# Expert batches of 6, 5, 3 and 2 groups in units of 128 rows, with seven weight slots, in a GNN and mixture-of-experts layer

## What is computed

```python
z = layernorm(x)
msg = z @ W + B
weights = where(adj < 1, exp(-(1/adj - 1)**2 / 0.5), 0)
x = x + weights @ msg
z = layernorm(x)
logits = z @ gate_w + gate_b
vals, idx = top_k(logits, 2)
share = softmax(vals)
h = relu(z @ w1[e] + b1[e])
expert_out = h @ w2[e] + b2[e]
y = z + sum(share * expert_out[idx])
x = x + layernorm(y) * gamma + beta
```

## Time and profile before

| what | value |
|---|---|
| median of three runs | 1759.18 us (1758.34 to 1759.6) |
| the profiled execution | 1758.88 us, its span 1757.1 us |
| PE, DVE, ACT, POOL busy | 92%, 87%, 90%, 24% of the span |
| aggregation until the last sum is copied | 0 to about 1470 us |
| tail | from there to 1757.1 us |
| rows loaded, a unit of 256 or of 128 | 128 KB in 2.1 us, 64 KB in 1.8 us from issue to landing |
| copy of one expert's weights | 493 ns, 120 times |

### The profile page before, as it was taken

How to read it: one execution, slowest core, us unless ns; L and a number is a source line. 1 busy time by engine, 2 the same in 40 slices (tenths; PEclk the granted TensorE clock), 3 DMA queues, 4 the chain that set the end, 5 groups by cost and what they waited for, 6 DMA issues and landing times.

```text
span 1757.1 us, 23405 instructions
## 1 busy us (share of the span) xinstructions
PE 1624.8 (92%) x8178; PEld 1080.6 (61%) x8178; DVE 1525.8 (87%) x2278; ACT 1581.2 (90%) x1577; POOL 430.1 (24%) x309
## 2 busy tenths in 40 slices
PE   4889999999999999999999999999999999999840
PEld 3556666566656566656556656566656557999840
DVE  7999999999999999999999999999999994557876
ACT  5889999999999999999989999999999995666752
POOL 0000030303131313131304030303031301117775
PEclk9999999999999999999999999999999999999985
DMA  9447876667666666666867666667666842457653
GB/s 319 146 136 252 251 213 205 187 203 217 200 203 199 195 204 204 202 200 201 230 192 207 203 207 204 189 202 216 203 188 203 230 123 77 149 156 227 193 152 97
DMA packets 208500, 341.91 MB, mean 195 GB/s; under 512 B 18224, under 2 KB 65840, under 8 KB 208256
## 3 DMA queue, kind: packets, MB, share of 16 engines
q1 hardware_dynamic: 200064, 323.30, 61.9%
q0 software_dynamic: 8320, 17.12, 3.2%
HBM read 304.38 MB, written 35.98 MB: 194 GB/s over the span
## 4 chain that ended last, share of the span: by engine, by line
PE 44%; ACT 28%; DVE 12%; issue 11%; POOL 4%; DMA 1%; POOLq 0%; SPq 0%; DVEq 0%; ACTq 0%
PE acc L1033 22%; PE tp L1052 11%; ACT chunk L467 10%; ACT chunk L462 9%; ACT wT L473 8%; PE tp L1082 4%; PE tp L1095 4%; POOL chunk L446 4%; DVE chunk L595 4%; DVE chunk L589 4%; PE tp L1071 1%; PE misc L985 1%; DVE stats L601 1%; DVE msg L650 1%; DMA xs<-in_x_dram 1%
## 5 line engine op out<-in xcount | busy, mean ns | idle before, releaser
L1033 PE MATMUL acc<-wT,msg 128*128 128x512 f32 x2048 | 973.0, 598 | 16.2 <-DVE yT L681 16.2
L595 DVE SCALAR_TENSOR_TENSOR chunk<-chunk 128x2048 f32<-128x2048 f32 x256 | 585.6, 2287 | 98.2 <-ACT chunk L467 98.0
L1052 PEld LDWEIGHTS tp<-ident,chunk 128*128 128x128 f32 x4096 | 484.1, 142 | 226.2 <-issue 214.7
L473 ACT ACTIVATE wT<-tp 128x1024 f32<-128x1024 f32 x512 | 570.4, 1114 | 22.4 <-PE tp L1052 22.4
L589 DVE SCALAR_TENSOR_TENSOR chunk<-chunk 128x2048 f32<-128x2048 f32 x256 | 584.0, 2282 | 1.9 <-DMA chunk<-in_adj_dram 1.9
L1052 PE MATMUL tp<-ident,chunk 128*128 128x128 f32 x4096 | 538.5, 275 | 0.0
L462 ACT ACTIVATE chunk<-chunk 128x2048 f32<-128x2048 f32 x256 | 514.9, 2011 | 11.9 <-DVE chunk L589 11.9
L1033 PEld LDWEIGHTS acc<-wT,msg 128*128 128x128 f32 x2048 | 351.6, 192 | 267.7 <-issue 267.0
L467 ACT ACTIVATE chunk<-chunk 128x2048 f32<-128x2048 f32 x256 | 513.7, 2007 | 0.0
L418 POOL TENSOR_TENSOR pool_carrier<-pool_carrier 1x1 f32<-1x1 f32 x32 | 8.6, 270 | 1232.0 <-DVE row_now L766 1189.5
L428 POOL DMA_INDIRECT rows_in<-y,row_now x128 | 286.6, 2239 | 44.7 <-issue 44.7
(11 more groups left out here) (106 smaller groups left out, 574.8 us busy)
## 6 DMA issues: line engine op xcount, KB each, us to landing
chunk<-in_adj_dram SPq DMA_DIRECT2D x256, 1024.0 KB, 5.3
chunk<-rows_in SPq DMA_DIRECT2D x88, 128.0 KB, 2.1
rows_out<-chunk SPq DMA_DIRECT2D x88, 128.0 KB
y_kept<-y SPq DMA_DIRECT2D x16, 256.0 KB, 6.1
rows_in<-zeros SPq DMA_DIRECT2D x32, 128.0 KB
chunk<-y_kept SPq DMA_DIRECT2D x16, 256.0 KB, 3.4
out_dram<-chunk SPq DMA_DIRECT2D x16, 256.0 KB, 2.6
blobs<-in_L_ffn_w_dram SPq DMA_DIRECT2D x1, 2048.0 KB, 12.0
```

The source lines that it names most:

```text
L473: act.activation(wT[:, (g * PPG + m) % WSLOTS, :], tp[(g * PPG + m) % TSLOTS][:, :], ACT.Exp, scale=-2.0).then_inc(weighted, 1)
L595: dve.scalar_tensor_tensor(out=slot(c), in0=slot(c), scalar=2.0, in1=slot(c), op0=ALU.subtract, op1=ALU.mult).then_inc(squared, 1)
L1033: ins = pe.matmul(acc[:, :], msg[:, n, :], wT[:, (g * PPG + m) % WSLOTS, k * ROWS:(k + 1) * ROWS], start=(n == 0), stop=(n == 2 * PPG - 1))
L1052: ins = pe.transpose(tp[s % TSLOTS][:, t * ROWS + b * P:t * ROWS + (b + 1) * P], chunk[:, c % RING, b, j:j + P], ident[:, :])
```

## The change

The batches become 6, 5, 3 and 2 groups, all in units of 128 rows, and each batch has 15 spare units for partly filled ones instead of 16. There are seven weight slots and weights are copied five units ahead, twelve slots for loaded rows instead of eight, and six result slots instead of four. The last group's gate takes a step only in every second round; its table begins in round 55, its pads in round 74. Groups are combined from 14 rounds behind a batch's last unit on, eleven rounds apart. Since a batch's number of units is no longer a multiple of the result slots, the wait for the results counts each slot's stores by itself.

```diff
--- before.py
+++ after.py
@@ -41,15 +41,15 @@
 
 
 
-    BATCHES = (8, 6, 2)
-    TILES = (2, 2, 1)
+    BATCHES = (6, 5, 3, 2)
+    TILES = (1, 1, 1, 1)
     UR = [t * P for t in TILES]
     UW = max(UR)
     FIRST = [sum(BATCHES[:b]) for b in range(len(BATCHES) + 1)]
     assert FIRST[-1] == GROUPS
     REGION = [n * ROWS + u for n, u in zip(BATCHES, UR)]
     BASE = [sum(E * r + u for r, u in zip(REGION[:b], UR)) for b in range(len(BATCHES) + 1)]
-    UNITS = [K * n * ROWS // u + E for n, u in zip(BATCHES, UR)]
+    UNITS = [K * n * ROWS // u + E - 1 for n, u in zip(BATCHES, UR)]
     UNIT0 = [sum(UNITS[:b]) for b in range(len(BATCHES) + 1)]
     NU = UNIT0[-1]
     MOST = max(UNITS)
@@ -134,7 +134,7 @@
         e_tab = sb("e_tab", [1, NU], I32)
         r_tab = sb("r_tab", [1, NU], I32)
 
-        SLOTS, RIN, RT, HT, RO, BACK, ZS, FIN = 4, 8, 3, 3, 4, 4, 3, 2
+        SLOTS, RIN, RT, HT, RO, BACK, ZS, FIN = 7, 12, 3, 3, 6, 4, 3, 2
         ring = chunk[:, :, :, :].rearrange("p r b j -> p (r b j)")
 
         def carve(start, n, width):
@@ -229,20 +229,16 @@
         MISC = 4
         SETUP_MISC = 2
 
-        def batch_at(i):
-            return max(b for b in range(len(BATCHES)) if UNIT0[b] <= i)
-
-
-        GATE_PACE = 1
-        TABLE_AT, PADS_AT = 28, 47
+
+        GATE_PACE = 2
+        TABLE_AT, PADS_AT = 55, 74
         TAIL_TABLES = len(BATCHES) - 1
-        COMBINE_WAIT, COMBINE_PACE, COMBINE_LONG = 8, 6, 10
+        COMBINE_WAIT, COMBINE_PACE, COMBINE_LONG = 14, 11, 10
         starts = []
         for b, n in enumerate(BATCHES):
             for _ in range(n):
                 at = UNIT0[b + 1] + COMBINE_WAIT
-                pace = COMBINE_PACE if starts and UR[batch_at(starts[-1])] > P else COMBINE_LONG
-                starts.append(max(at, starts[-1] + pace) if starts else at)
+                starts.append(max(at, starts[-1] + COMBINE_PACE) if starts else at)
         LAST = starts[-1] + COMBINE_LONG + 2
 
         def batch_of(u):
@@ -431,7 +427,7 @@
 
             def results_there(b):
                 for i in range(RO):
-                    pool.wait_ge(ro_out[i], UNIT0[b + 1] // RO * 16)
+                    pool.wait_ge(ro_out[i], (UNIT0[b + 1] - i + RO - 1) // RO * 16)
 
             for b, n in enumerate(BATCHES):
                 for g in range(FIRST[b], FIRST[b + 1]):
@@ -945,14 +941,14 @@
                     dve.tensor_tensor(fin[g % FIN], z, rows(xs, g), ALU.add).then_inc(fin_ready, 1)
 
             dve.wait_ge(turned, (GROUPS - 1) * PPG + PPG - RING // 2 * PAIRS)
-            for u in range(2):
+            for u in range(SLOTS - 2):
                 fetch(u)
             gate_sum(GROUPS - 1)
             for i in range(LAST):
                 if 1 <= i <= NU:
                     add_bias(i - 1)
-                if i + 2 < NU:
-                    fetch(i + 2)
+                if i + SLOTS - 2 < NU:
+                    fetch(i + SLOTS - 2)
                 if i % GATE_PACE == 0:
                     gate_slot(GROUPS - 1, i // GATE_PACE)
                 table_slot(len(BATCHES) - 1, i - TABLE_AT)
```

## The result

The change makes the kernel slower: 1769.76 us, median of four runs (1768.24 to 1773.7), against 1759.39 (1758.34 to 1759.76) for the kernel before beside it. The ratio is 1.0065 [1.0049, 1.0081]. The prediction was 1752 us, range 1741 to 1764, so the time lies outside the range and on the other side of no change. The profiled execution took 1768.24 us, its span 1766.3.

What follows compares the result with a forecast made beforehand. The tail was taken as bound by sync queue and VectorE, both without room: first bias 1477.4, last bias 220 us later at 1697.4, 52.5 us of combine, 1.8 outside the span: 1752 us, range 1741 to 1764.

Steps and rivals of the forecast that it cites:

- part 3: Tail units: the sync queue's 1.00 us per unit plus table reads and pads sum to F + 212.3.
- F: Time of the tail's first bias, forecast at 1477.4 us; later tail times are counted from it.
- Part 1: Tables built in the aggregation, three batches' instead of two: 3.8 us more in sum, 2 to 6 kept.
- Part 2: Start of the tail: half as tall a tile takes about 1.0 us off before the first bias (0 to 2).
- The interference of 3.5 us: Tail units: sync queue and VectorE, each without room, lose 3.5 us to each other; last bias F + 220.
- VectorE's own pace: Tail units with the combine beside them: 13.0 us per 11 units, 1.18 each; last bias F + 216.4.
- Part 4: Tail: gathers start at 1551, 21 us sooner; 52.5 us remain after the last bias, without waiting for gathers.
- gathers were not starved: Against the rival that every VectorE copy blocks GpSimd 0.49 us: gathers end 1784, program near 1799 us; chance 0.02.
- Results that return too slowly: Rival, tail: stores take 6.5 us to land, so six slots hold biases back; F + 237.7, 1769 us; chance 0.13.
- The queue overlaps: Rival, tail: the queue hides; TensorE's 75.2 us to round 73, then 1.12 per unit; F + 202, 1734 us; chance 0.15.
- No change: Rival: tables cost 6 us, queue and VectorE cost each other 8; 1759 us; chance 0.18.
- three signs of being wrong: Tail: queue under 1.00 us per round, biases waiting 6 us for stores, or the last combine group waiting for its gather.

Runs made afterwards that it cites:

- e1: The changed kernel with twelve result slots instead of six; 1765.24 us, ratio 1.0038 to the kernel before.
- e4: The changed kernel with the last batch's 16 pads in rounds 57 to 72 instead of 74 to 89; 1767.86 us, ratio 1.0064 to the kernel before.
- f1: e1 with the results of two neighbouring units in one store of 128 KB; 1745.21 us, ratio 0.9934 to the kernel before.
- f2: f1 with a transfer of 512 bytes for each left-out store; 1756.66 us, ratio 0.9998 to the kernel before.
- f4: f1 with a combine group every nine rounds instead of 11; 1746.76 us, ratio 0.9932 to the kernel before.

## Why the prediction was wrong

**What bounds the kernel, and where to look: right.** The aggregation kept TensorE's pace, and only the tail decided. The step that failed is the queue's own sum in part 3, F + 212.3 for the store of unit 181, which was issued at F + 236.8. Against the span of 1749.9 the profiled one is 16.4 longer: F came 6.4 us sooner (1471.0 for 1477.4), the units took 23.3 us more (F + 243.3 for F + 220), and the rest 0.5 less.

**Part 1, tables: too dear.** Forecast 3.8 us more, measured -2.3. The first table cost 4.1 us where 5.4 was forecast, that of group 12 3.0 for 4.4, and the last two groups gave 0.4 back where I had 1.4 of cost. Another 1.3 us was already there at the first sum, and is not the change's. One profile cannot tell more: in six profiles of kernels with this aggregation (after, e1, e4, f1, f2, f4) the last sum is copied between 1468.33 and 1473.87, mean 1470.7.

**Part 2, first bias: right.** 1.3 us sooner for a forecast of 1.0.

**Part 3, the queue's own sum: wrong, and the cause of the miss.**

| the queue's round | forecast | store issued |
|---|---|---|
| 73 (unit 72) | F + 78.4 | F + 86.8 |
| 89 (unit 88) | F + 106.1 | F + 117.5 |
| 182 (unit 181) | F + 212.3 | F + 236.8 |

The unit's 1.00 and the pad's 0.53 us were right. Two terms were not. The long issues were put at nothing: 20 of them add 16 us. The table reads were put at 0.87 us, 13 times, from a load of 1.21 us that was in truth one of the long issues. They are instructions of their own in the gap ahead of a load:

```profile
L332 SPq TENSOR_LOAD <-r_tab x15: 278/1033/2132, 1442.4 to 1687.3; - x15
```

The three figures are the least, the median and the longest in ns. 14 of these and one for the pads lie in the units. There are more than the multiples of 16 give, since each batch begins with a read too. With their gaps they take 17 us, where 11 was forecast. The two terms together are 22 of the 24.5 us; waits for results before that store are 3.3, and six rounds without a load give 1.8 back.

Both costs stood in the trace of the kernel before, with 8 long issues and reads of the same length. They cost nothing there, because that queue spent 77.9 us waiting for results.

**The interference of 3.5 us: not what failed.** The queue lost 1.2 us to VectorE up to unit 177 and 5.9 in the last stores. VectorE lost 24.4 us to the queue, but that is the queue's pace reaching it through six slots. With twelve, the queue's work stayed at 238 us and so did the length of the units. With half the stores it fell to 218.0 - 33.1 = 184.9 us and the last bias came at F + 218.0. VectorE's own pace was nearly right: 1.18 a unit forecast, 1.215 measured in f1, where the queue has room, and last bias F + 218.0 against my F + 216.4.

**Part 4, gathers and combine: right in the main, partly by luck.** GpSimd started at 1548.2 for 1551, but by two errors that cancel: the last store of the first batch was issued at F + 74.1, not F + 67, and released GpSimd 3.1 us later, not 6.5. It paused between batches (17.2 us before the second), and the rest after the last bias took 52.0 for 52.5 us with one wait of 2.1 for a gather. That gathers were not starved is right too: five groups from 1548.18 to 1602.16 took 10.80 us each, against the 10.91 and 10.34 of the earlier trace rows (10.88 and 10.40 from marker to marker). The rule of the Trainium skill, "SBUF — State Buffer", section "SBUF: two separate sides", can have cost some 0.4 us a group here at most.

**The rivals.** *Results that return too slowly* gave 1769 us, and bias 89 at F + 108.8 (measured F + 108.7). The number is right by luck: the stores seen to hold a bias landed within 1.9 to 4.6 us of their issue, not 6.5, but were issued up to 10 us after the result. *The queue overlaps* fell with the 1.00 us between stores. *No change* let queue and VectorE cost each other 8 us, where 7.1 were the queue's waits, but took the queue's sum as I did. None of the rivals, and none of my three signs of being wrong, asked what happens if a round costs the queue more than its count.

## What to carry to other kernels

A queue's sum is more than transfers times the usual issue. Here reads of a table and now and then a long issue added 33 us to some 200. Such costs are free while the queue waits for results and are paid in full once it has no room, so count them in the rows of the kernel before. Halving a tile doubles the issues of the queue while the work stays the same; merge neighbouring transfers (two results in one store) first. A wait that more buffers remove may only move; ask which stream is late, not which buffer is empty. And before you believe that a late stream also waits, pair each of its instructions with the one it needs.

## What was not expected of the hardware

- In these runs the queue's cost went by the transfer, not by its bytes: a store of 128 KB holds it as long as one of 64 KB (0.42 to 0.43 us, then 0.2 until the next), one of 512 bytes little less (0.31), and two loads in a row 0.85.
- Some issues of the same transfers take 0.7 to 2.0 us. There were 20 in the tail after, 8 in the tail before; what they are is open, and no run took them away.
- On one chip every kernel was 105 to 133 us slower, the four profiled ones in the tail alone, with TensorE stopped for up to 8 us at a time, and the gain of the pairs did not show on it: f1's kernel gained 0.66% elsewhere and lost 0.17% there.
- TensorE's clock fell to 1.2 GHz five times within the units of the kernel after and never in those of f1, but its falls did not set the time.
